# A decoder layer on one core: the first half of the query product moved in front of the scores, two banks exchanged, the last turns written out

## What is computed

```python
x = x + attn(layernorm(x))              # 16 heads, RoPE on q and k, causal, over T = 128
x = x + xattn(layernorm(x), ctx)        # q = qdq(x) @ qdq(wq).T + bq; out = qdq(o) @ qdq(wp).T + bp
x = x + ffn(layernorm(x))               # router softmax, top 8 of 64, rows into 64 x 128 slots,
                                        # silu(gate) * up, down, weighted sum back to the tokens
# qdq(x): s = max|x| / 127 per row; clip(round(x / s), -127, 127) * s
```

## Time and profile before

| | before |
|---|---|
| median of 3 runs | 1690.42 us (1682.73 to 1698.85) |
| profiled execution, its own time | 1691.19 us |
| its span | 1689.4 us |
| PE, DVE, ACT, POOL busy | 84%, 70%, 56%, 43% of the span |
| granted TensorE clock, mean | 0.935 |
| first 160 us | weights, constants, the first rounds |
| 160.62 to 1163.66 us | 27 rounds |
| to 1292 us | the last rounds; rows of the last scatter land |
| 1292 to 1689 us | expert stage |

### The profile page before, as it was taken

One profiled execution on the slowest core, in us unless ns is written; L12 is line 12 of the kernel. 1 busy time (PEld: TensorE's weight loads), 2 busy tenths in 40 slices (PEclk: granted clock), 3 DMA queues, 4 the chain that ended last, 5 costly groups with the idle time before them and its releaser, 6 DMA issues.

```text
span 1689.4 us, 36382 instructions
## 1 busy us (share of the span) xinstructions
PE 1414.6 (84%) x11243; PEld 1061.0 (63%) x11276; DVE 1179.7 (70%) x3050; ACT 944.6 (56%) x3313; POOL 734.6 (43%) x718
## 2 busy tenths in 40 slices
PE   5499898998878999898999998889854988888895
PEld 3377676776666677766777676667642655555564
DVE  4878787888777888888888878877752444444453
ACT  2367666766656776666776656656741333333332
POOL 2123444444443454445354445334442444555565
PEclk9599999999999999999999999999976999999997
DMA  6755322222211110111110110110087999999964
GB/s 198 298 203 214 124 100 93 92 91 102 94 44 36 33 37 31 31 56 31 31 37 31 37 50 31 31 31 26 14 272 246 273 274 273 275 278 284 281 102 52
DMA packets 164529, 204.33 MB, mean 121 GB/s; under 512 B 40245, under 2 KB 122421, under 8 KB 164480
## 3 DMA queue, kind: packets, MB, share of 16 engines
q1 hardware_dynamic: 125568, 165.86, 29.8%
q0 software_dynamic: 38912, 37.87, 11.0%
HBM read 136.19 MB, written 130.29 MB: 158 GB/s over the span
## 4 chain that ended last, share of the span: by engine, by line
DVE 26%; PE 21%; DMA 19%; issue 17%; another core or an unknown queue 7%; ACT 5%; POOL 1%; DVEq 1%; POOLq 0%; SPq 0%; ACTq 0%
DMA out<-x,slots 19%; PE bank L525 10%; ACT probs L990 3%; DVE small L1257 3%; PE bank L531 3%; PE bank L553 3%; DVE small L1290 2%; DVE chosen L1354 2%; DVE wide_a L1326 2%; PE bank L507 2%; DVE roped L1323 1%; DVE x L1333 1%; DVE wide_b L1498 1%; PE bank L560 1%
## 5 line engine op out<-in xcount | busy, mean ns | idle before, releaser
L990 ACT ACTIVATE probs<-bank,small 128x128 f32<-128x128 f32 x1024 | 362.8, 384 | 127.7 <-DVE small L1290 101.3
L1783 POOL DMA_INDIRECT routed<-row,slots x248 | 257.5, 1038 | 130.8 <-issue 74.2
L1738 POOL TENSOR_TENSOR small<-small,half 128x1 f32<-128x1 f32 x96 | 54.2, 565 | 544.6 <-DVE small L1262 543.5
L1858 POOL DMA_INDIRECT out<-x,slots x128 | 198.4, 1550 | 197.5 <-DMA out<-x,slots 146.1
L990 ACT ACTIVATION_READ_ACCUMULATOR probs<-bank,small 128x1 f32 x1024 | 229.7, 224 | 0.0
L984 ACT ACTIVATE probsT<-bank 128x512 f32<-128x512 f32 x256 | 144.1, 612 | 108.2 <-PE bank L553 89.8
L1290 DVE TENSOR_REDUCE small<-bank 128x4 f32<-128x512 f32 x256 | 166.6, 683 | 46.4 <-remote 38.7
L553 PE MATMUL bank<-idf,probs 128*128 128x128 f32 x1024 | 155.6, 287 | 4.7 <-ACT probs L990 3.1
L553 PEld LDWEIGHTS bank<-idf,probs 128*128 128x128 f32 x1024 | 126.9, 150 | 35.6 <-issue 8.8
L1693 DVE TENSOR_SCALAR slots<-pairs 128x1 uint32<-128x1 f32 x128 | 13.7, 149 | 188.8 <-DMA out<-x,slots 181.8
L525 PE MATMUL bank<-w_k_hi,xT_hi 128*128 128x512 f32 x128 | 63.9, 499 | 49.2 <-ACT xq8T L984 30.6
(11 more groups left out here) (248 smaller groups left out, 3943.6 us busy)
## 6 DMA issues: line engine op xcount, KB each, us to landing
w_gate_up<-in_w_gate SPq DMA_DIRECT2D x128, 192.0 KB
w_gate_up<-in_w_up SPq DMA_DIRECT2D x128, 192.0 KB
w_down<-in_w_down SPq DMA_DIRECT2D x128, 192.0 KB
routed<-empty_row SPq DMA_DIRECT2D x16, 1280.0 KB, 11.7
x_in<-in_x SPq DMA_DIRECT2D x32, 256.0 KB
xn<-in_xT_in SPq DMA_DIRECT2D x32, 256.0 KB
ctx_sb<-in_ctxT_in SPq DMA_DIRECT2D x32, 256.0 KB
x_res<-in_x SPq DMA_DIRECT2D x32, 256.0 KB
```

Source lines behind the costliest of these rows:

```text
L990: last = act.activation(probs[:, g, j * P:(j + 1) * P], bank[:, b, j * P:(j + 1) * P], ACT.Exp, bias=negated[:, h:h + 1], **({"accum_out": ...
L1738: pool.tensor_tensor(c["r0"], c["v"], half[:, :], ALU.pow).then_inc(g_pow[kind], 1)
L1783: pool.indirect_dma_start(routed, bass.IndirectOffsetOnAxis(ap=slots_of(m)[:, k:k + 1], axis=0), row_of(m)[:, :], None, bounds_check=SLOTS ...
L1858: pool.indirect_dma_start(out.rearrange("b p (h c) -> (b p h) c", h=2), bass.IndirectOffsetOnAxis(ap=place_of[k % 2][:, half_:half_ + 1], ...
```

## The change

On PE, the body has `queries_a` directly in front of `self_scores`; `queries_b` stands where `queries_a` stood, `queries_c` where `queries_b` stood, and nothing stands in front of `cross_scores`. The turned cross attention goes to bank 5 and the turned quantised x to bank 1; the waits follow the banks: `queries_a` waits for `e_kT` of the tile before, `keys_a` for `d_xatt`. `self_scores` waits for step 2 of `find_slots` in place of step 6, and `cross_scores` for the first of the two steps of `second_sum`. SP issues the weights of experts 0 to 4 two rounds after the loop without waiting for `p_xk` and `p_o`, those of 5 to 7 a round later. The last rounds are written out by hand: PE from round B + 3, ACT, DVE and POOL from B + 4.

```diff
 # PE
             def self_scores(m):
-                reached(pe, d_r2, m - 3, 6, 6)
+                reached(pe, d_r2, m - 3, 6, 2)
             def turn_cross_attention(m):
-                turn(4, xatt, p_xo)
+                turn(5, xatt, p_xo)
             def turn_quantised_x(m):
-                turn_bf16(5, xq8, p_q8T)
+                turn_bf16(1, xq8, p_q8T)
             def queries_a(m):
                 reached(pe, g_xT, m, 2, 1)
-                reached(pe, d_xatt, m - 3, 2, 2)
+                reached(pe, e_kT, m - 1, 1, 1)
             def keys_a(m):
-                reached(pe, a_q8T, m - 2, 1, 1)
+                reached(pe, d_xatt, m - 3, 2, 2)
             def cross_scores(m):
-                reached(pe, d_x2, m - 1, 2, 2)
+                reached(pe, d_x2, m - 1, 2, 1)
 # PE, body
+                    queries_a(cur - 1)
                     self_scores(cur - 2)
...
                     cross_values_a(cur - 3)
-                    queries_a(cur - 1)
+                    queries_b(cur - 1)
                     keys_a(cur - 1)
...
                     cross_queries(cur - 3)
-                    queries_b(cur - 1)
+                    queries_c(cur - 1)
...
                     turn_probs_0(cur - 2)
-                    queries_c(cur - 1)
                     cross_scores(cur - 3)
 # SP, after the loop
                 if cur == B + 2:
-                    for projected in (p_q, p_k, p_v, p_xk, p_o):
+                    for projected in (p_q, p_k, p_v):
                         sp.wait_ge(projected, 3 * B)
-                    for k in range(2):
+                    for k in range(5):
+                        load_weights(k, k)
+                if cur == B + 3:
+                    for projected in (p_xk, p_o):
+                        sp.wait_ge(projected, 3 * B)
+                    for k in range(5, 8):
                         load_weights(k, k)
                 if cur == B + 4:
-                    for k in range(2, 8):
-                        load_weights(k, k)
 # PE, tail from B + 3 (a part)
+            cross_queries(B)
+            cross_values_a(B)
+            turn_quantised_o(B - 1)
+            turn_cross_queries(B)
+            cross_output(B - 1)
+            cross_scores(B)
+            turn_cross_probs_1(B)
+            turn_cross_probs_0(B)
+            turn_normed(B - 1)
+            turn_cross_probs_2(B)
+            turn_cross_probs_3(B)
+            weigh_turned(5, 1, xv_sb, p_xpv)
 # ACT, tail: four exponentials with nothing between; copies of groups 2 and 3 only
+            cross_exp_1(B)
+            cross_exp_2(B)
+            cross_exp_3(B)
 # DVE, tail (a part): the norm of tile 31, two copies of turned probabilities, one of x3T
+            dve.tensor_scalar(row_of(B - 1)[:, 0:D], x2[:, :], ln["ffn"]["r"], ffn_shift, ALU.mult, ALU.add).then_inc(a_normed, 1)
+                dve.tensor_copy(probsT[:, g, :], bank[:, b, :]).then_inc(a_xpT, 1)
+            dve.tensor_copy(x3T[:, :], bank[:, 3, :]).then_inc(a_x3T, 1)
+            cross_average(B)
+            scale_o(B)
+            router_max(B - 1)
+            round_o(B)
+            quantise_o(B)
+            route(B - 1)
+            shares(B - 1)
+            find_slots(B - 1)
+            second_sum(B)
 # POOL, tail
+            scatter(B - 1, 0, 2)
+            ffn_power(B)
+            scatter(B - 1, 2, TOPK)
+            scatter(B)
```

72 lines of the change are left out of this document (63 added, 9 removed).

## The result

The changed kernel takes 1737.91 us (median; 1732.91 to 1742.92) beside 1686.58 for the kernel before on the same chip: 1.031 of it, 95% interval 1.026 to 1.036. The forecast was 1691 (1668 to 1714), no change. The profiled execution has a span of 1731.1 us against 1689.4, 41.7 more. The 27 rounds alone have 42.2 more, 1045.28 against 1003.04.

What follows compares the result with a forecast made beforehand. A loop round was taken as bound by a ring of waits over the scatter, 35.75 us. From the profiled 1691.19 us, +6 for the loop's clock and -6.2 for the tail gave 1691, range 1668 to 1714.

Steps and rivals of the forecast that it cites:

- The floor: A loop round at full granted clock takes 35.75 us, and the change leaves that as it is.
- a ring: From find_slots' end over scatter, turned probabilities' copy and second_sum to the next find_slots' end: 0.86, 11.98, 2.91, 20.00 us.
- (a) of the loop: queries_a fills PE's hole before the scores, delaying them 0.1 to 0.6 us; cost nothing, up to 0.6 without cover.
- the term of 2.91 us: From ACT's copy of the turned probabilities, through copies and cross_output, to second_sum; left at 2.91 us.
- the four rounds in which the copy came at the end: Four loop rounds of about 41 us, 5.3 each above 35.75; effect taken as 0, bounds -21.2 and +21.2.
- The looser wait: The scores' wait for step 2 of find_slots buys nothing, as queries_a in front keeps them from beginning earlier.
- Rival E: Scores get ahead of the scatter, their signals aren't late, a round loses two or three us: 1620; chance 0.02.
- (b): Wait before old queries_a (1.23 us) goes; keys_a starts about 651.4, not 653.92; turn_probs_1 stays at 655.32, no gain.
- (c): Hole before cross_scores: 0.93 us of PE's time is freed in which nothing can begin; cost and gain nothing.
- The clock: PE's idling nearly all in one piece: 17 of 22 rounds at 1.2 us, less 14.3, gives +6.
- Rival A: One 2.7 us idle piece costs the clock in every ordinary round; 1712, prices 1695 to 1725; chance 0.20.
- The tail: Hand-written last rounds: -2.6 up to the cross scores, -3.3 to the last product, -0.3 to the last scatter; sum -6.2.

Runs made afterwards that it cites:

- the variant: The change with the first queries piece directly before the second, behind cross_values_a, not before the scores; 1661.81 us, 0.983 of the kernel before.
- the front placement alone: The change with only the first queries piece moved before the scores, the second and third in their old places; 1797.86 us, 1.064 of the kernel before.
- the second trace of the change: The changed kernel run again unaltered, where the kernel before takes 1660.33 us; 1685.70 to 1712.77 us in four executions, 1.015 to 1.032.

## Why the prediction was wrong

**The floor.** Right: 35.75 us a round is a ring over the scatter, and the change doesn't touch it. Rounds at clock 1.00 took 35.4 to 36.0 us before, with the change, and in its variants with eight descriptors in one run started at the usual place, but for four of 34.8 to 35.3 (three of them the loop's first, one with a late second descriptor).

**The step that failed is (a) of the loop**: "0.1 to 0.6 later [...] Cost nothing", with the cover that "DVE takes the scores only at 648.86, some 2.4 us after they are done". The delay was sized right (0.18 us against the scatter), its price was not: it is some 37 us in the 27 rounds, from 1008.05 in the kernel with the queries closed up behind cross_values_a under the old wait to 1045.28 in the change. In the ring it is the term of 2.91 us, from the copy of the turned probabilities to second_sum, which the prediction left as it was: it became 5.44 in the round shown. The 2.4 us were not slack. They were the wait in the line of PE's signals, and whoever joins the line later makes all that follows later: the copy of the turned x by 1.4 us, turn_probs_1 past the end of the scatter, and with it PE's chain to cross_output. The prediction had seen both halves, signals late behind the scatter and the four rounds in which the copy came at the end, and treated the place in the line as fixed.

**The looser wait** "buys nothing". For the change that is right, as queries_a ends later than find_slots (937.14 + 0.40 against 937.05 + 0.18). As a step it was the strongest part: with the queries closed up and nothing in front of the scores it takes the lead from 0.80 to 1.44 and is worth 33 us of the rounds, where before takes 1685. Rival E named this race. What stood against it ("the scores begin later, not earlier") was right for the change, but it was not turned round: the prediction didn't ask what the later start would cost. E's price was wrong too: signals out ahead of the scatter leave the floor as it is (1662, not 1620).

**(b) and (c).** turn_probs_1 "stays at 655.32" failed with (a). The freed 0.93 us in front of cross_scores were put at nothing. At clock 1.00 that holds (35.55 in the kernel before with step 2, 35.55 in the variant). At 0.95 the round is 37.13 in the one and 36.16 in the other; from second_sum to the next find_slots' end, the stretch in which DVE needs the cross scores, it is 20.92 us in the one and 20.06 in the other (medians of 27). That the queries in front of cross_scores are the cause fits this, but no run moved them alone.

**The clock.** Forecast +6 from the shape of the pauses; with the old wait, closing up alone gave +5.0 us (about 9 in the medians). That agrees in size, which is partly luck: more of its rounds also have a late copy (12 above 8 us, 9 before), so the clock's own part isn't separated. The prediction had counted late copies as lost clock: of its thirteen rounds at 0.91 to 0.95, five have the copy at 8.0 to 8.8 us behind the scatter's start and hold 9.2 of the 14.3 us, the dearest (38.23) among them; the other eight cost 0.63 each, not 1.10. Rival A had the sign, but its prices end at 1725, and 25 of 27 rounds did lose the clock, but not by its cause: the variant has the same closed-up queries and loses 0.6 us in a round with clock 0.95. PE's pause of 3.46 us and the fallen clock are what the late copy does next. The Trainium skill, page "TensorE: Matmul & The Clock Gate", section "HAM oscillation — how this bites in real kernels", has it that a TensorE which waits between bursts of work is throttled and pays at the next burst. The trace agrees for that turn_probs_1, with 1.12 us at a granted clock of 0.50 behind the pause.

**The tail.** Forecast -6.2, measured -0.7. The part behind the cross scores gained 2.8 of 3.6. The part ahead of them lost it again: the wait for the store went, and cross_output's signal then waited for the scatter of tile 30: cross_output ends at 1282.86, its signal arrives at 1285.44. It is the same line of signals, forgotten in the same way.

Left open: why a lead of 0.62 gives copies at 7.3 us in some rounds of the first trace and at 8.7 or 10.2 in others; whether the issue of the descriptors or the writing of their rows holds the signals; and what makes the kernel before take 1685 us in some runs and 1658 in others. The chips with 1685 were used first and those with 1658 later, none of them for both, so that it is the chip is not shown.

## What to carry to other kernels

A wait that ends "remote" or late with nobody busy is not slack: ask what the line is and who joins it when, before moving work in front of the one that joins. Where two things race (here the scores' signals and the scatter's start), write down the lead in the trace and what the change does to it, to a tenth of a microsecond. And when a reordering loses, run its parts: here, where the kernel before takes 1685 us, two parts of one edit were worth -2% and +6%, and the gain of the one was invisible under the loss of the other.

## What the runs showed of the hardware

During a scatter of eight indirect descriptors (10 us) PE's signals reached the other engines late by up to 9 us (a turn done at 530.95, copied at 540.02 with the front placement alone), one by one and then, about 1.4 us behind the last descriptor, together (eight within 0.5 us in the round of the earlier trace rows). DVE's signals reached PE and ACT at once in the same stretch (in the change's round shown, xatt is done at 944.14 and PE goes on at 944.19; the maximum is done at 942.36 and ACT goes on at 942.40). With one descriptor, or while the second one came late, PE's signals were not held (copy at 3.8 us; 32.0 us a round with one descriptor). In the second trace of the change 0.11 us less lead (0.62 to 0.51) moved the copy from some 7.2 to 11.5 us in six of nine rounds. And one kernel, the one before, took 1685 us on some chips and 1658 on others, where the change took 1738 and 1686 to 1713; the gain of a variant (0.983) in the one case was none (0.9995) in the other.
